# Routing the first expert part in two halves and folding the attention weights between its tiles

## What is computed

```python
x = x + 0.5 * ffn(layernorm(x))      # expert part 1
x = x + attention(layernorm(x))      # 8 heads of 64, keys and values from a 64-wide latent
x = x + 0.5 * ffn(layernorm(x))      # expert part 2

def ffn(x):                          # 8 experts, one per token
    logits = x @ gate_w.T
    sel, rw = argmax(logits), sigmoid(max(logits))
    for e in range(8):
        xs = x * (rw * (sel == e))[:, None]
        out += (xs @ w_up[e].T) * silu(xs @ w_gate[e].T) @ w_down[e].T
```

## Time and profile before

| what | us |
|---|---|
| runs | 1071.90, 1071.98, 1072.31 |
| profiled execution | 1074.65 |
| its span | 1072.8 |
| TensorE busy | 960.4 (90%) |
| VectorE busy | 700.3 (65%) |
| GpSimd busy | 686.5 (64%) |
| ScalarE busy | 475.4 (44%) |

### The profile page before, as it was taken

One profiled execution on the slowest core, in us unless ns is written; L12 is line 12 of the kernel. 1 busy time (PEld: TensorE's weight loads), 2 busy tenths in 40 slices (PEclk: granted clock), 3 DMA queues, 4 the chain that ended last, 5 costly groups with the idle time before them and its releaser, 6 DMA issues.

```text
span 1072.8 us, 14511 instructions
## 1 busy us (share of the span) xinstructions
PE 960.4 (90%) x5024; PEld 515.9 (48%) x5024; DVE 700.3 (65%) x1139; ACT 475.4 (44%) x765; POOL 686.5 (64%) x392
## 2 busy tenths in 40 slices
PE   6279966997999989999999999999999999896995
PEld 4168732443444454444445544444454444355884
DVE  4845468566778674776776566777666668676663
ACT  4824431443434435444543454444324444634663
POOL 0055350486989916677774577678637778885775
PEclk9679957798999999999999999999999999998998
DMA  9435421026011010000001000000100030005441
GB/s 328 157 108 160 131 74 69 6 78 176 11 15 16 11 69 1 1 1 1 1 1 69 1 1 1 1 1 1 69 2 1 1 118 1 1 34 189 138 140 48
DMA packets 39733, 59.92 MB, mean 56 GB/s; under 512 B 5866, under 2 KB 33518, under 8 KB 38640
## 3 DMA queue, kind: packets, MB, share of 16 engines
q1 hardware_dynamic: 17664, 25.14, 7.0%
q0 software_dynamic: 8736, 17.91, 6.1%
q10 hardware_dynamic: 13264, 15.97, 4.4%
HBM read 27.50 MB, written 25.85 MB: 50 GB/s over the span
## 4 chain that ended last, share of the span: by engine, by line
PE 64%; DVE 19%; POOL 7%; ACT 3%; issue 3%; DMA 2%; ACTq 1%; POOLq 0%; SPq 0%; DVEq 0%
PE ps_o L1290 15%; PE ps L1277 10%; DVE maxes L1113 8%; PE ps L1107 8%; PE ps L843 7%; DVE rows_store L1664 5%; PE ps_x L1087 5%; POOL arena_b L1766 4%; PE ps L1439 3%; PE ps_x L1312 3%; PE ps L827 2%; PE ps_o L859 2%; PE ps_x L859 1%; ACT rows_store L761 1%; DMA x_res<-x_in 1%
## 5 line engine op out<-in xcount | busy, mean ns | idle before, releaser
L1113 DVE TENSOR_REDUCE maxes<-ps 128x2 f32<-128x1024 f32 x256 | 310.7, 1217 | 196.9 <-PE ps L1107 196.3
L1766 POOL TENSOR_TENSOR arena_b<-arena_b 128x1024 f32<-128x1024 f32 x112 | 272.3, 2437 | 178.6 <-PE ps_o L1290 142.7
L1766 POOL TENSOR_TENSOR arena_b<-arena_b,hot_store 128x1024 f32<-128x1024 f32 x108 | 262.8, 2433 | 68.2 <-PE ps_o L1290 35.0
L1277 PE MATMUL ps<-q_split,keys_now 64*128 64x512 f32 x1536 | 205.3, 392 | 0.0
L1523 ACT ACTIVATE arena_b<-ps 128x1024 f32<-128x1024 f32 x144 | 143.3, 1023 | 101.6 <-PE ps L1277 101.6
L1277 PEld LDWEIGHTS ps<-q_split,keys_now 64*128 64x128 f32 x1536 | 145.3, 186 | 32.9 <-issue 4.1
L1290 PE MATMUL ps_o<-arena_b,latent_now 128*64 128x512 f32 x576 | 148.2, 616 | 1.3 <-ACT arena_b L1523 1.3
L1523 ACT ACTIVATE hot_store<-ps 128x1024 f32<-128x1024 f32 x112 | 112.0, 1022 | 57.5 <-PE ps L1277 57.5
L1290 PE MATMUL ps_o<-hot_store,latent_now 128*64 128x512 f32 x448 | 116.0, 614 | 2.5 <-ACT hot_store L1523 2.5
L1664 DVE RECIPROCAL rows_store<-rows_store 128x256 f32<-128x256 f32 (+1 forms) x72 | 112.6, 1564 | 6.5 <-ACT rows_store L1534 6.5
L1107 PE MATMUL ps<-keys_max_now,q_split 64*128 64x512 f32 x384 | 94.1, 486 | 7.6 <-DVE maxes L1113 6.4
(11 more groups left out here) (325 smaller groups left out, 1138.3 us busy)
## 6 DMA issues: line engine op xcount, KB each, us to landing
sorted_y<-arena_b ACTq DMA_DIRECT2D x40, 128.0 KB, 2.0
x_res<-sorted_x SPq DMA_DIRECT2D x32, 130.0 KB, 2.4
x_res<-x_in SPq DMA_DIRECT2D x4, 1024.0 KB, 13.8
scaled_x<-rows_store SPq DMA_DIRECT2D x16, 256.0 KB, 2.1
keys_now<-keys_next SPq DMA_DIRECT2D x4, 1024.0 KB, 4.5
sorted_x<-blank ACTq DMA_DIRECT2D x2, 1560.0 KB, 13.0
sorted_x<-blank ACTq DMA_DIRECT2D x2, 1430.0 KB, 10.2
arena_a<-w_gu SPq DMA_DIRECT2D x1, 2048.0 KB, 14.3
```

The source lines that it names most:

```text
L1113: nc.vector.tensor_reduce(maxes[:, 2 * m:2 * m + 2], bank[:, :, :], AX_X, ALU.max) \
L1277: last = nc.tensor.matmul(ps_s[n % 2][:, a, :], keys_now[h, key, k], query[h, p, q], start=False, stop=(kt >= KT - STRIDE and query is q_h ...
L1766: nc.gpsimd.tensor_tensor(t, t, prob(k, kt).rearrange("p a n -> p (a n)"), ALU.add) \
```

## The change

- All of expert part 1 is routed in two halves of 16 token tiles each, with 23 slot tiles per half. `SLOT_TILES` goes from 40 to 46. `scaled_x` and `sorted_y` become two DRAM tensors each, one per half.
- The first half is routed as soon as its logits are there, with the `_late` functions of part 2; the columns of groups 6 and 7, the logits of the last two groups and the sums of the last load come between or behind its steps. The second half is routed inside the tile steps, by three functions named `inside`, one per engine.
- The fold is done inside the tile steps too, one head per step from step 18 to 25. It has one bank for `w_qk` (5) and one for `w_vo` (7). So hidden transposes have only bank 4 and `down` only bank 6.
- The gathers of token tiles 0 to 15 wait only for the first half's stores, and VectorE adds rows 0 to 6 in steps 43 to 49.
- The bf16 copies of two tables (`ones_h`, `before_h`) move from behind the fold to ScalarE's start.

```diff
-SLOT_TILES = NT + EXPERTS
+SLOT_TILES = SLOT_TILES_2
+BACK_AT = SLOT_TILES - 3
+RANKS_AT = 1
+TOKENS_AT = 10
+FOLD_AT = 18
...
 pe_router
-            for g in range(LOADS):
...
-            logits_of(GROUPS - 2)
...
+            logits_of(2)
+            turn(5)
+            back(0)
+            logits_of(4)
+            pe_ranks_late(pe, "f1a", AHEAD)
+            pe.wait_ge(sem("x_loaded3"), 16)
+            turn(6)
+            turn(7)
+            pe_tokens(pe, 0)
+            logits_of(6)
             back(1)
...
 act_router
+            for q in range(4):
+                columns(q)
+            copy_rows(0)
+            act_std(act, "f1", 0, AHEAD)
+            columns(4)
+            columns(5)
+            act_exp_top_late(act, "f1a", 0, AHEAD)
+            for n in range(AHEAD_PAIRS):
+                act_scaled_pair(act, n)
+            columns(6)
+            columns(7)
+            act_hot_id(act, 0)
             copy_rows(1)
+            act_std(act, "f1", AHEAD, NT, 1)
...
 dve_router
+            dve_scale(dve, "f1", 0, AHEAD, 0)
+            dve.wait_ge(sem("masks"), 3)
+            dve_logits(dve, 0)
+            dve_one_hot_late(dve, "f1a", 0, AHEAD)
+            dve.wait_ge(sem("x_tail"), 2)
+            dve_weight_late(dve, "f1a", 0, AHEAD)
+            dve_starts_late(dve, "f1a", 0, AHEAD, 0, small[:, 5, :])
+            dve.wait_ge(sem("tables"), 3)
+            dve_slots_late(dve, "f1a", 0, AHEAD)
+            dve_hot_hi(dve, 0)
+            dve_hot_lo(dve, 0, 0)
+            dve_hot_lo(dve, 0, 1)
+            stats_of(3)
+            dve_tokens(dve, 0)
+            dve_codes_early(dve, "f1", small[:, 5, :])
+            dve_variance(dve, "f1", AHEAD, NT)
...
+        def pe_fold(pe, n):
+            p, a = n // 2, n % 2
+            h = slice(a * HD, (a + 1) * HD)
+            if n == 0:
+                pe.wait_ge(sem("raw_loaded"), 64)
+                pe.wait_ge(sem("token_of_f1"), 2)
+            else:
+                pe.wait_ge(sem("fold_copied"), 2 * n)
...
+        def act_fold(act, n):
...
+            act.wait_ge(sem("folded"), 2 * n + 1)
+            nc.scalar.activation(w_qk[:, :, p, h], banks[5].rearrange("p (c n) -> p c n", c=DC)[:, :, 0:HD],
+                                 ACT.Copy).then_inc(sem("fold_copied"), 1)
+            act.wait_ge(sem("folded"), 2 * n + 2)
+            nc.scalar.activation(w_vo[h, p, :], banks[7][h, 0:D], ACT.Copy).then_inc(sem("fold_copied"), 1)
...
 pe_experts
+                if FOLD_AT <= t < FOLD_AT + HEADS:
+                    pe_fold(pe, t - FOLD_AT)
+                if t == RANKS_AT:
+                    pe_ranks_late(pe, "f1b", AHEAD)
+                if t == TOKENS_AT:
+                    pe_tokens(pe, 1)
...
 act_experts
+                if FOLD_AT < t <= FOLD_AT + HEADS:
+                    act_fold(act, t - FOLD_AT - 1)
+                if t == 1:
+                    act_exp_top_late(act, "f1b", AHEAD, NT)
+                if 2 <= t < 2 + AHEAD_PAIRS:
+                    act_scaled_pair(act, AHEAD_PAIRS + t - 2)
+                if t == TOKENS_AT - 1:
+                    act_hot_id(act, 1)
...
 dve_experts
+                if t == -2:
+                    dve_scale(dve, "f1", AHEAD, NT, 1)
+                elif t == -1:
+                    dve_logits(dve, 1)
+                    dve_one_hot_late(dve, "f1b", AHEAD, NT)
+                elif t == 2:
+                    dve_weight_late(dve, "f1b", AHEAD, NT)
+                elif t == 3:
+                    dve_starts_late(dve, "f1b", AHEAD, NT, 0, small[:, 6, :])
+                elif t == 4:
+                    dve_slots_late(dve, "f1b", AHEAD, NT)
+                elif t == 5:
+                    dve_hot_hi(dve, 1)
+                elif t in (6, 8):
+                    dve_hot_lo(dve, 1, (t - 6) // 2)
+                elif t == TOKENS_AT + 1:
+                    dve_tokens(dve, 1)
+                elif t == TOKENS_AT + 2:
+                    dve_counts_late(dve, small[:, 5, :], small[:, 6, :])
+                elif t == TOKENS_AT + 4:
+                    dve_codes_late(dve, "f1")
+                elif BACK_AT <= t:
+                    dve_gathered(dve, (t - BACK_AT) // RING, (t - BACK_AT) % RING)
...
 pool_gather
-            for k in range(RING):
-                pool.wait_ge(sem(f"y_stored{k}_f1"), 16 * (SLOT_TILES // RING))
+            for t in range(AHEAD_TILES - RING, AHEAD_TILES):
+                sent, count = y_sent(t)
+                pool.wait_ge(sent, count)
...
 tensor
-            for p in range(PAIRS):
-                for a in range(2):
-                    h = slice(a * HD, (a + 1) * HD)
-                    if p:
-                        pe.wait_ge(sem("fold_copied"), 4 * (p - 1) + 2 * a + 2)
```

More of the change, by code:

```diff
@@ L303, in copy_rows, with columns @@
                 nc.scalar.activation(logit_rows[:, n, :], banks[6 + n], ACT.Copy).then_inc(sem("logit_rows_copied"), 1)
-            for q in range(GROUPS):
+            def columns(q):
                 for c in range(DC):
@@ new lines, in dve_hot_lo, with dve_tokens @@
+        def dve_hot_lo(dve, h, part):
+            t0 = h * AHEAD + part * QT
+            lows = [P, QT, P]
+            nc.vector.tensor_tensor(hot_lo[:, t0:t0 + QT, :], st[:, 2, t0:t0 + QT].unsqueeze(2).to_broadcast(lows),
+                                    count_p[:, :].unsqueeze(1).to_broadcast(lows), ALU.is_equal) \
+                .then_inc(sem("hot_lo_f1"), 1)
+        def dve_tokens(dve, h):
+            dve.wait_ge(sem("tokens_f1"), h + 1)
+            parts = banks[4 + h][:, 0:2 * AHEAD_TILES].rearrange("p (a h) -> p a h", a=2)
+            in_tile, ids = (scratch(SPACE["f1b" if h else "f1a"][1], n * AHEAD_TILES, AHEAD_TILES) for n in range(2))
@@ L782, in pool_sorted_rows, with pe_tokens @@
-        def pool_sorted_rows(pool, tag):
-            for k in range(RING):
-                pool.wait_ge(sem(f"stored{k}_{tag}"), 16 * (NT // (2 * RING)))
-            pool.wait_ge(sem(f"token_of_{tag}"), 1)
-            for t in range(SLOT_TILES):
-                k = t % RING
+        def pe_tokens(pe, h):
+            pe.wait_ge(sem("hot_id_f1"), 2 * h + 2)
+            for i in range(AHEAD):
+                if i % QT == 0:
+                    pe.wait_ge(sem("hot_lo_f1"), 2 * h + i // QT + 1)
+                last = nc.tensor.matmul(banks[4 + h][:, 0:2 * AHEAD_TILES], hot_lo[:, h * AHEAD + i, :],
+                                        hot_id[:, h, i, :, :].rearrange("p a h -> p (a h)"),
+                                        start=(i == 0), stop=(i == AHEAD - 1))
+            last.then_inc(sem("tokens_f1"), 1)
@@ L934, in tile @@
                         store(t - LAG - 1, (k - LAG - 1) % RING)
+                    inside(t)
                 else:
@@ L1485, in act_attention @@
             act.wait_ge(sem("row_scale_att"), 2)
+            for t in range(SLOT_TILES - RING, SLOT_TILES):
+                sent, count = y_sent(t)
+                act.wait_ge(sent, count)
             def batch(b):
```

405 lines of the change are left out of this document (159 added, 246 removed).

## The result

The changed kernel takes 1085.05 us (median of 4 runs, 1082.51 to 1087.53), the kernel before 1072.14 in the same session (1071.9 to 1072.31): a ratio of 1.012, 95% interval 1.0097 to 1.0144. The profiled execution has a span of 1083.6 us (before 1072.8).

What follows compares the result with a forecast made beforehand. Steady tiles run at TensorE's pace, and none starts until all token tiles are routed. Start -12.5, six more tiles +9.8, route +9.1, folds +16.8, end -10.1 sum to +13.1: 1071.98 becomes 1085 us, range 1074 to 1100.

Steps and rivals of the forecast that it cites:

- Start: Ahead of the tiles: first gate and up at 47.9 us instead of 60.4, -12.5 us.
- Route: Second half's route inside the tile steps exceeds VectorE's spare time and makes TensorE wait, +9.1 us.
- Folds: Eight folds inside tile steps: 9.3 us of TensorE work plus 7.5 of waits for ScalarE's copies, +16.8 us.
- Single banks: Tile steps: one bank each for `down` and the hidden transposes costs nothing.
- End: From last gate and up to eighth row: about 8.4 us instead of 18.5, -10.1 us.
- The table loads: Three added on ScalarE, 1.28 us each by the trace; the skill's 2.66 would make the sum 4 us higher.
- this rival: Fold steps: the clock falls, a step takes 5.9 us against 3.9, 1099 us in all; chance 0.20.
- Folds paid, waits not: Rival, fold steps: folds cost their work but not the 7.5 us of waits, 1077.6 us; chance 0.08.
- The head start: Rival, ahead of the tiles: half as long, first gate and up at 54, 1091 us; chance 0.10.

Runs made afterwards that it cites:

- e1: Changed kernel with the eight folds put back behind the tiles, on pairs of banks in turn; 1087.4 us, ratio 1.0137 to the kernel before.
- e7: Changed kernel with the second half's route in every second step, up to step 17, instead of steps 2 to 14; 1087.16 us, ratio 1.0139.
- e2: Changed kernel with one fold in every second step, steps 18 to 32, its copies one step behind; 1079.29 us, ratio 1.0061 to the kernel before.
- e10: e9 with route codes in step 15, rows back and folds two steps earlier, attention's square root in step 45; 1068.79 us, ratio 0.9961.
- e5: Changed kernel with two banks for `down`; second half's ranks and all fold products in bank 5; 1084.85 us, ratio 1.0114 to the kernel before.
- e3: Changed kernel with TensorE's register load of expert numbers ahead of `down` instead of behind it, in both parts; 1085.35 us.
- e4: Kernel before with one bank for `down` in its first expert part; 1080.07 us, ratio 1.0062 to the kernel before.
- e9: Changed kernel with two `down` banks, fold and row-back add every second step from 30, earlier attention square root, e7's route; 1072.47 us, ratio 1.0003.

## Why the prediction was right

The median lies within 0.1 us of the forecast, and of the signs that it named all but one came out: first gate and up at 47.05 (48 said), 19.7 us to tile 8 (21), steps of 3.73 and 3.87 us in turn (3.9), eighth row 7.5 us behind the last gate and up (8), a clock of 1.00 between 95 and 125 us, 1.0 us of change behind the eighth row (under 2). The one is TensorE's wait for the copy of `w_vo`, 0.7 to 0.8 us where 1.1 was said. (The 14.6 us that it gives for tiles 0 to 8 before are 14.3 in the trace.) Point by point:

- **Start.** Right to 0.9 us, or 0.4 against the other traces of the old start. The chain was the one named: ScalarE late with `hot_id`, then TensorE's last logits. It is a term with a spread that the prediction didn't give: by e1 and e7 the same code can start its tiles 2.1 us earlier, where the clock is up during the third logits.
- **Route.** Mis-sized, +7.5 instead of +9.1. The mechanism is as named: `starts` in step 3 stops VectorE for 3.1 us, and TensorE waits 1.74. e7 shows that part of it fits into the spare time if spread.
- **Folds.** +16.7 for +16.8, but its split was off: TensorE waits 5.2 us, not 7.5 (e2 gave back 5.8). The step is right all the same, because ScalarE's copies set it: in step 20 they are done 2.66 us behind the start of gate and up (2.7 forecast) and the fold takes 1.16, which makes 3.87. Where the forecast had TensorE at the fold after 1.63 us, it is there after 1.89, so it works or stalls 0.26 longer and waits 0.25 less. Steps 19 to 25 take 26.5 us in all (27.0 forecast), and step 18, without a wait, 3.18 (2.8), of which 0.3 is the load of the next point. What the prediction didn't say is that the folds had no free place to go back to. e1 shows them as dear behind the tiles, once the rows back are early. The end's -10.1 and the folds' +16.8 belong together in the two orders of e1 and of the changed kernel; e2 and e10 show that a third order has the end for less, a fold in every second step.
- **Single banks.** Wrong for `down`, right for the hidden transposes (e5 keeps their single bank and its steps are 1.63). "The single banks for `down` and the hidden transposes cost nothing" looked at the data alone: `y_out` is done 0.4 us before `down` is due. But behind the wait the register load that follows costs 0.5 us in each fourth step (e3, e4, e5), 2.2 us in steps 26 to 45 and 0.3 in step 18. The route's 1.6 too many made up for it.
- **End.** Right to 0.9.
- **The table loads.** The row's 1.28 us, with the next operation 0.02 behind, was enough. In e1 the square root follows its load at 155.78, 0.01 us after the load ends, and no drain shows. The Trainium skill's 2.66 us for a switch (ScalarE: Activation LUTs, What ACT_TABLE_LOAD costs) would have put the sum 4 us too high.
- **The rivals.** The clock did not fall in the fold steps: TensorE waits 0.7 to 0.8 us in each of seven and keeps 2.4 GHz. The Trainium skill's case of a loop that is throttled again every turn (TensorE: Matmul & The Clock Gate, HAM oscillation) is not this one: its loop waits for a DMA in each turn, several times as long as the 1.07 us that the prediction reckoned with. So the prediction went too far when it said that the section would make this rival the forecast. "Folds paid, waits not" is what e2 then made. The head start was whole.

That the sum hit so closely is partly luck. In the two profiled executions the misses (-0.9, -1.6, +2.2, -0.9, -1.0) leave 2.3 us, of which the late start of the kernel before is 1.1 to 1.4; and the runs of the changed kernel lie 5 us apart. With the changed kernel's start as it is in e1 and e7, the span would have been another 2.1 us shorter.

## What to carry to other kernels

Work that is hidden has a cover, and a change that removes the cover can put the work onto the path in its old place as well as in its new one, as e1 shows: price both together, and look on every engine for what stands behind it in order (here a square root behind eight copies). A small job inside a pipelined loop costs its own length plus a wait if it needs its own last result in the same turn; put it in every second turn. A wait that ends shortly before its engine would need it can still cost, if a register load stands behind it: put the load ahead of it (e3).

## What the runs showed of the hardware that I had not expected

- A register load on TensorE behind a `down` that waits for the `y_out` just before it shows as 0.47 us of idle time put down to "issue"; with `down` on two banks (e5) or the load ahead of `down` (e3), the same load shows nothing in this part.
- TensorE idle for 2.32 us came back at 1.2 GHz in e7 and at 2.4 GHz in e9 (2.31 us), in the same step of the same route.
- Attention's stretch of identical work lasts 825.9 us where the clock granted 10 to 25 us behind its first transposes is 0.96, and 829.5 to 829.8 where it is 0.71 or 0.72; between these the order is not strict. A gain of 2 us ahead of it (e5) can vanish in it, and only comparing the two places in the trace shows that it was made.
- The same code can start at another clock in another execution: the third logits of the changed kernel's start take 3.50 us in one and 1.91 in another, and the tiles begin 2.1 us apart.
